# Layer-norm variances of a 512-column chunk held as eight rows of 64 columns instead of four rows of 128

## The reference

```
def _layernorm(x, axis=-1, eps=1e-05):
    m = jnp.mean(x, axis=axis, keepdims=True)
    v = jnp.var(x, axis=axis, keepdims=True)
    return (x - m) / jnp.sqrt(v + eps)

x = x + 0.5 * L0_ffn(_layernorm(x))       # coupled FFN, three cycles
x = x + L0_attn(_layernorm(x))            # causal attention, 16 heads, ends in a norm with gamma and beta
x = x + 0.5 * L0_ffn(_layernorm(x))
x = x + 0.5 * L1_ffn(_layernorm(x))       # router, 8 experts, top 2
x = x + L1_attn(_layernorm(x))            # full attention, 16 heads
x = x + 0.5 * L1_ffn(_layernorm(x))
```

## Time and profile before

| | us |
|---|---|
| three runs | 1341.12, 1344.8, 1364.45 |
| median | 1344.8 |
| the profiled execution, its own time | 1350.28 |
| its span, first to last instruction | 1348.4 |
| its busy time: PE / PEld / DVE / ACT / POOL | 1298.8 / 470.6 / 1162.3 / 1056.3 / 184.2 |
| its mean granted TensorE clock | 0.977 of full speed |

### The profile page before, as it was taken

One profiled execution on the slowest core, in us unless ns is written; L12 is line 12 of the kernel. 1 busy time (PEld: TensorE's weight loads), 2 busy tenths in 40 slices (PEclk: granted clock), 3 DMA queues, 4 the chain that ended last, 5 costly groups with the idle time before them and its releaser, 6 DMA issues. The chain is left out here.

```text
span 1348.4 us, 30323 instructions
## 1 busy us (share of the span) xinstructions
PE 1298.8 (96%) x11960; PEld 470.6 (35%) x11960; DVE 1162.3 (86%) x1536; ACT 1056.3 (78%) x2060; POOL 184.2 (14%) x463
## 2 busy tenths in 40 slices
PE   7889999999999998999899999999999999999998
PEld 4343333332333352555222222222222222223554
DVE  6877989999999177766899999999999999998465
ACT  4657888998999736434499999999999999999732
POOL 9234221111111200112000000000000000000100
PEclk9989999999999999899599999999999999999999
DMA  5251301200000012001411000000000000000000
GB/s 133 53 144 36 61 6 24 56 5 13 4 4 4 13 29 66 1 0 56 109 50 51 4 3 12 4 3 4 12 4 4 3 4 12 4 4 3 12 8 24
DMA packets 38526, 35.10 MB, mean 26 GB/s; under 512 B 16081, under 2 KB 31921, under 8 KB 38385
## 3 DMA queue, kind: packets, MB, share of 16 engines
q1 hardware_dynamic: 38384, 33.17, 10.1%
HBM read 17.03 MB, written 9.70 MB: 20 GB/s over the span
## 5 line engine op out<-in xcount | busy, mean ns | idle before, releaser
L1523 DVE TENSOR_REDUCE m_blockmax<-ps 128x2 f32<-128x1024 f32 (+1 forms) x768 | 880.3, 1207 | 25.6 <-PE ps L1344 16.6
L1496 ACT ACTIVATE m_prob<-ps 128x512 f32<-128x512 f32 (+3 forms) x1664 | 845.6, 576 | 48.9 <-PE ps L1382 35.8
L1382 PE MATMUL ps<-m_q_max,m_k_all 64*128 64x512 bf16 (+3 forms) x1664 | 339.5, 369 | 0.7 <-ACT m_prob L1496 0.4
L1344 PE MATMUL ps<-m_k_all,m_q_all 64*128 64x512 bf16 (+3 forms) x1664 | 318.7, 381 | 19.1 <-DVE m_blockmax L1523 14.8
L1405 PE MATMUL ps<-m_prob,m_v_op 128*9 128x256 f32 x4096 | 317.8, 382 | 0.1
L1344 PEld LDWEIGHTS ps<-m_k_all,m_q_all 64*128 64x128 bf16 x1664 | 79.7, 93 | 350.7 <-DVE m_blockmax L1523 179.6
L1401 PE MATMUL ps<-m_prob,m_v_op 128*9 128x256 f32 (+3 forms) x2560 | 178.6, 352 | 0.9 <-ACT m_prob L1496 0.3
L1382 PEld LDWEIGHTS ps<-m_q_max,m_k_all 64*128 64x128 bf16 x1664 | 143.6, 94 | 92.5 <-ACT m_prob L1496 47.9
L1547 POOL CAST m_maxparts<-m_negmax 128x8 bf16<-128x8 f32 x64 | 14.1, 221 | 718.0 <-DVE m_negmax L1531 712.2
L1405 PEld LDWEIGHTS ps<-m_prob,m_v_op 128*9 128x9 f32 x4096 | 60.9, 88 | 132.7 <-issue 115.8
L803 ACT ACTIVATE m_prob<-ps 128x512 f32<-128x512 f32 x40 | 23.9, 597 | 68.9 <-PE ps L667 55.5
(11 more groups left out here) (226 smaller groups left out, 1079.3 us busy)
## 6 DMA issues: line engine op xcount, KB each, us to landing
m_part<-m_xn SPq DMA_DIRECT2D x48, 128.0 KB, 2.3
ba_parts<-m_part SPq DMA_DIRECT2D x8, 384.0 KB, 4.2
ea_parts<-m_part SPq DMA_DIRECT2D x8, 384.0 KB, 2.6
m_k_all<-ea_parts SPq DMA_DIRECT2D x84, 32.0 KB
m_q_all<-ea_parts SPq DMA_DIRECT2D x84, 32.0 KB
m_k_all<-ba_parts SPq DMA_DIRECT2D x36, 64.0 KB
m_q_all<-ba_parts SPq DMA_DIRECT2D x36, 64.0 KB
ba_sums<-m_pv SPq DMA_DIRECT2D x128, 9.0 KB
```

The source lines that it names most:

```text
L1344: mm = pe.matmul(ps[:, MX + 2 * (u % 2) + j, 0:width], q_all[head, pair, q0:q0 + TW], k_all[head, pair, CW * kc:CW * kc + width], start=Tr ...
L1382: pe.matmul(ps[:, e % ST, q0:CW], k_all[head, pair, TW * i:TW * i + TW], q_max[m % 2][head, q0:CW], start=True, stop=True).then_inc(self.s ...
L1496: nc.scalar.activation(prob[:, (2 * t + j) % NP, q0:CW], ps[:, e % ST, q0:CW], ACT.Exp, scale=SCALE)\
L1523: nc.vector.tensor_reduce(blockmax[:, m % plan.AHEAD, qt, :, kc], ps[:, MX + 2 * (u % 2):MX + 2 * (u % 2) + 2, 0:width], AX.X, ALU.max)\
```

## The change

A chunk's variances lie as eight rows of 64 columns. `pe_var` makes eight products of 64 columns instead of four of 128, and so does `pe_spread`; `act_root` and `dve_invert` work on 32 x 64 instead of 32 x 128. `var_of` and `row_of` have eight slices instead of four, and the width of a slice of `row_of` stays 128, the partitions that are written.

```diff
+VROWS = 8
+VCOLS = CW // VROWS
...
-        k["var_of"] = n.sb("var_of", [P, TPC, 32], fp32)
-        k["row_of"] = n.sb("row_of", [32, TPC, TW], fp32)
+        k["var_of"] = n.sb("var_of", [P, VROWS, 32], fp32)
+        k["row_of"] = n.sb("row_of", [32, VROWS, P], fp32)
...
-        for u in range(TPC):
+        for u in range(VROWS):
             nc.vector.memset(k["var_of"][:, u, u:u + 1], 1.0 / P)
...
         pool.affine_select(out=k["row_of"][:, :, :], in_=k["row_of"][:, :, :], compare_op=ALU.not_equal, fill=1.0,
-                           base=0, pattern=[[-1, TPC], [0, TW]], channel_multiplier=1).then_inc(made, 1)
+                           base=0, pattern=[[-1, VROWS], [0, P]], channel_multiplier=1).then_inc(made, 1)
...
-        for u in range(TPC):
-            mm = pe.matmul(self.ps[0:32, bank, 0:TW], self.k["var_of"][:, u, :], tile(self.k["sq"], TPC * c + u),
-                           start=(u == 0), stop=(u == TPC - 1))
+        for u in range(VROWS):
+            mm = pe.matmul(self.ps[0:32, bank, 0:VCOLS], self.k["var_of"][:, u, :],
+                           chunk(self.k["sq"], c)[:, VCOLS * u:VCOLS * u + VCOLS], start=(u == 0), stop=(u == VROWS - 1))
...
-        for u in range(TPC):
-            mm = pe.matmul(tile(self.ps[:, bank, :], u), self.k["row_of"][:, u, :], self.std[:, c, :],
+        for u in range(VROWS):
+            mm = pe.matmul(self.ps[:, bank, VCOLS * u:VCOLS * u + VCOLS], self.k["row_of"][:, u, :], self.std[:, c, :],
                            start=True, stop=True, skip_group_check=True)
...
-        self.nc.scalar.activation(self.std[:, c, :], self.ps[0:32, bank, 0:TW], ACT.Sqrt, bias=self.k["eps"][0:32, 0:1])\
+        self.nc.scalar.activation(self.std[:, c, :], self.ps[0:32, bank, 0:VCOLS], ACT.Sqrt, bias=self.k["eps"][0:32, 0:1])\
...
-        k["std"] = n.sb("std", [32, NC, TW], fp32)
+        k["std"] = n.sb("std", [32, NC, VCOLS], fp32)
```

## The result

| | before | changed | the profiled execution: before | changed |
|---|---|---|---|---|
| median us (range, runs) | 1349.88 (1341.12 to 1364.45, 6) | 1401.63 (1393.5 to 1411.08, 6) | 1350.28 | 1393.5 |
| span us | | | 1348.4 | 1391.7 |
| mean granted clock | | | 0.977 | 0.968 |

The changed kernel takes 1.0387 times as long as the kernel before (95% interval 1.0346 to 1.0427), 3.9% more. The forecast was 1372 us, with 1386 as its upper end. So the direction was right, and the size wrong by some 29 us. About 5 us of these are the base: the forecast was laid on the median of three runs, 1344.8 us, and over six it is 1349.88. The added time is 51.75 us against 27.5, and the missing 24 us are what is to be explained.

A forecast was written before the change was run, and what follows sets the result against it. PE was taken as the bound in the norm stages; 24.9 + 1.7 + 0.9 - 0.5 - 1.2 + 1.7 = 27.5 us on the 1344.8 us median gave 1372 us. Its own range was 1362 to 1384, with other cases 1352 to 1386.

The forecast's parts named there:

- The spread, +24.9: PE's spread passes in the norms: 16 instead of 8 a chunk, each as long as before, +24.9 us over 28 chunks.
- The variance, +1.7: PE's variance passes in the norms: 16 a chunk at 0.057 us, +0.06 us a chunk, 1.7 us in all.
- The table at the start, +0.9: Kernel start: PE's first product waits for POOL's select on the wider `row_of`; memset and select grow, +0.9 us.
- Root and reciprocal, -0.5: Norms: reciprocal 0.39 us and root about 0.08 us shorter a chunk, mostly where nobody is late, so -0.5 us.
- Cover that swallows some, -1.2: Start of the causal loop: earlier-starting transfers hide between 0 and 1.8 us of the added time, taken as -1.2 us.
- The clock, +1.7: TensorE in dense spreads: halved moving columns bring one fall to half speed of some 3.3 us, costing 1.7 us.
- the clock falls often: Rival, chance 0.15: clock falls at all eight places with dense spreads, sum 39.4 us, 1384 us.
- The columns case: Rival, chance 0.07: spread passes with half the moving columns are half as long, about 1345 us, not slower.
- the half-hidden case: Rival, chance 0.16: PE isn't the bound at half of the places, half of the 24.9 us hidden, 1360 us.
- The sign that I had named for being wrong: In the profile after, among other signs: the clock row has three or more new stretches at 0.5.

The follow-up runs named there:

- e2: The kernel before with its four spread products of 128 columns issued twice; 1396.38 us, 1.0345 of before.
- e5: e2 with std and row_of on all 128 partitions, zeros in the added rows; 1368.68 us, 1.013 of before.
- e7: The kernel before with std and row_of on all 128 partitions, zeros in the added rows; 1344.97 us, 0.995 of before.
- e4: The kernel before with root and reciprocal on 64 of the 128 columns, half of the tokens getting a wrong factor; 1349.07 us, 1.0009 of before.
- e10: The changed kernel with std and row_of on 64 partitions instead of 32; 1394.15 us, 1.0314 of the kernel before.
- e8: e7 with the variance's weights 128 columns wide in place of 32; 1341.03 us, 0.9914 of the kernel before.
- e9: The changed kernel with std and row_of on all 128 partitions, zeros in the added rows; 1370.72 us, 1.0145 of the kernel before.

## Why the prediction was wrong, point by point

- **The spread, +24.9: right.** A pass takes 0.111 us with 64 columns. Between groups it came to 1.92 - 1.08 = 0.84 a chunk at LN_B, 23.5 in all, since the gap at a change of weight shape is in the old distance as well as in the new one and a little smaller in the new. e2, which is this term alone, leaves 1350.2 - 1326.0 = 24.2 us with half of the time at half speed taken off; e5 against e7 gives 23.7.
- **The variance, +1.7: right, a little less.** 0.055 us a pass gives 16 x 0.055 = 0.88 against 0.85, +0.03 a chunk; the timeline has +0.02. Below 1 us in all.
- **The table at the start, +0.9: right**, 0.88. The select was 1.08 us.
- **Root and reciprocal, -0.5: not contradicted.** The reciprocal takes 541 ns where 547 were worked out, and the root is 0.05 us shorter instead of 0.08. e4 shows what both are worth: 1.0009 of the time, 0.9965 to 1.0054, so a gain of 8 to 11 us is ruled out and half a us can't be told from nothing.
- **Cover that swallows some, -1.2: not tested apart.** With the terms above the sum is 23.5 + 0.6 + 0.9 - 0.5 - 1.2 = 23.3, and the runs without the clock's part say 23; so nothing large is missing, but 1 us can't be told.
- **The clock, +1.7: this step failed.** It measured about 28 us: some 57 us more at half speed. I took one fall of some 3.3 us, priced like the one in the earlier trace rows. The largest value that I let stand was eight of them, 13.6 us. In number that was enough, with two new stretches and two longer ones in the profiled execution. The bound failed in the length of a fall: 10, 10, 14 and 17 us, where the work that follows, spreads included, runs at half speed (3.67 us for the group that takes 1.99). And the cause that I named was only part of it. I compared moving columns, the router's 8 with the spread's 64, and overlooked what the same row shows as its first number: the spread has 32 rows. I also took 128 moving columns as the level that is safe. e2 has 128 and falls all the same, once its groups are twice as long: with 32 rows, groups of at most 16 passes (1.9 us) brought no stretch behind LN_A and LN_C, and groups of 32 (3.7 us) did. With 128 rows, groups of 32 brought none there either.

Of the rivals, "the clock falls often" was the nearest, but its 1384 us had the same price of a fall and the same cause in it. The columns case and the half-hidden case are out: of the work's 25 us some 23 came. The sign that I had named for being wrong, three or more new stretches at 0.5 in the clock row, isn't met by the letter: the row shows no digit 5 in the changed kernel, and the windows have two new stretches and two longer ones.

What stays open is what the chip weighs. Rows of the array that are in use, or the array's mode with less than 128 rows: e10 lies between. The added rows hold zeros and that is enough; no run had other numbers there. Nor do the runs show why some groups of 32 passes bring a fall and others don't.

## What to carry to other kernels

A pass whose cost is its weight load doesn't get cheaper with fewer moving columns, so to cut the columns in half and double the passes is a loss on PE, to be paid in full where PE is the bound. Before making a group of small passes longer, look at how much of the array they use: here groups of 32 passes on 32 or 64 partitions brought the clock to half while PE showed no idle time, and to lay the operands on all 128 partitions, with zeros, cost nothing in the passes. Groups that alternate between weight shapes pay a gap at each change; giving them one shape was worth 0.9% here (e8, with the full rows).

## What the runs showed of the hardware that I had not expected

- TensorE's clock fell from 1.00 to 0.50 while PE was busy for every microsecond (windows above). What changed the outcome was the rows of the array in use: 1396 to 1369 us (e2 to e5), 1401.6 to 1370.7 (the changed kernel to e9). The Trainium skill (TensorE: Matmul & The Clock Gate, HAM oscillation) has as its rule that PE must have no long idle gaps. The windows above show none ahead of the fall, so keeping that rule wasn't enough here.
- A change of weight shape between two groups cost 0.1 to 0.2 us at full speed: distances of 0.99 us (from 128 x 32 to 32 x 128) and 1.08 us (back) against 0.89 with one shape.
- A float32 pass with 32 columns of weights and 64 moving ones took 0.055 us (the changed kernel's variance), one with 128 columns of weights 0.111 whether 8 (router), 64 (changed kernel) or 128 columns (before) move.
